# Attention layers of a one-core kernel: the second half of the key projection moves from PSUM bank 7 to bank 4

## The chip, the cores and the metric

The kernel runs on one core of a Trainium2 chip. The metric is the device time of one execution in microseconds (us). TensorE (PE in the profile; its weight loads are PEld) does the matrix products and writes PSUM; VectorE (DVE), ScalarE (ACT) and GpSimd (POOL) do the rest; SyncE (SP) issues the transfers. PSUM is used here as eight banks of 128 x 512 float32, written `PS[:, bank, :]`.

## The reference

The input x is 64 sequences of 64 tokens of 256 channels. Four residual layers follow one another: two of attention with style modulation, then two state-space layers. The change touches the attention layers only:

```
x  = x * s1;  x = (x - mean(x)) * rsqrt(var(x) + 1e-5)
q, k, v = x @ q_weight.T * q_dc, x @ k_weight.T * k_dc, x @ v_weight.T * v_dc * s2
attn = softmax(q @ k.T * 16 ** -0.5)        # 16 heads of 16, 64 x 64 per sequence
x  = x + (attn @ v) @ w_weight.T * w_dc + v_flat @ u_weight.T * u_dc
```

## The kernel before, in words

Channels lie on the partitions, in two halves of 128 (`HC` = 2, index m or c). Tokens are worked in groups of 8 sequences, 512 tokens (one PSUM bank wide). There are 8 groups and two attention layers, so `body` runs 16 times; call the turns 0 to 15. Turns 1 to 4 are a loop on the chip that is entered twice with two bodies each time round, and so are 9 to 12; the others are written out. The two state-space layers come after turn 15 and are not touched.

Each engine has a written-out order, and semaphores hold the engines together. One turn of `body` on TensorE does, for group `it`: the outward projection of the group before; the turned values; the scores of the second half; then eight times "turn" (transpose a block of probabilities into PSUM, bank 4 for even k and bank 7 for odd k, `turn_bank`, line 253) and "weigh" (probabilities by values, bank 5). ScalarE copies each turned block to SBUF (`turned`, line 649). In the middle of these eight, TensorE prepares other groups:

- `mean_spread(it + 2, 7)` spreads the token means of group it + 2 into bank 7; VectorE subtracts them (`centred`, line 1347, tile xm). xm is complete when that bank has been read.
- the key projection of group it + 1 (`project(one, 1, m, ...)`, line 881): first half to bank 6, second half to bank 7. Since bank 7 holds the means until `centred` is through, the second half waits for xm.
- ScalarE reads each half twice, once for each parity of the heads (`keys`, line 637, tile kz), after it has done the exponent of the second half (line 653) and the squares of group it + 2 (line 625).
- the query projection of group it + 1: its halves go to banks 6 and 7 again, so each waits until `keys` has read that half's bank.
- `square_sums(it + 2, 6)`, the skip projection (line 881 on vsc, banks 2 and 3), `rstd_spread(it + 2, 7)`, `turn(it, 4)` and so on.

A float32 projection of one half is two matmul calls and shows as four matmul records in the trace ("x4"); both halves together are "x8". Turn 14 prepares no group it + 2 (there is no group 16), so there the second half of the keys has no xm to wait for. Turn 15 makes no projections of keys.

The last step of a turn is `project(one, 2, 1, ...)`, the second half of the values; ScalarE copies it, takes the exponent of the next group's first scores, and VectorE sums, scales and adds the residual of the group before (lines 1377 to 1410).

Of the kernel before, what the change touches and what calls it, by code (L numbers as in the profile page):

```python
# [14 lines left out]
HC, DC = H // P, DI // P  # L15
# [27 lines left out]
def cond_resid_kernel(nc, xT, condT, attw, win, wconv, chan, wxp, wdt, dtv, wout, dskip,  # L43
                      ident_d, spread_d, fold_d, masks_d, rowmask_d, ones_x, out):
    f32, bf16 = mybir.dt.float32, mybir.dt.bfloat16
    ALU, ACT, AX = mybir.AluOpType, mybir.ActivationFunctionType, mybir.AxisListType
# [15 lines left out]
    with es:  # L62
# [5 lines left out]
        def sb(name, shape, dt=f32, where=None):  # L68
            return (where or es).enter_context(nc.sbuf_tensor(name, shape, dt))

        PS = es.enter_context(nc.psum_tensor("PS", [P, 8, 512], f32))
# [13 lines left out]
        par = [masks[:, 0:1], masks[:, 1:2]]  # L85
# [23 lines left out]
        kz = sb("kz", [P, HC, 2, TOK], where=att)  # L109
# [141 lines left out]
        fin = sem("final")  # L251

        turn_bank = (4, 7) * 4
        AT = LAYERS * G
        USED, READY, KEPT, W0 = 16, 20, 2, 32
        Y_STORES = PASSES * (CHUNKS // 2) * 16
# [230 lines left out]
        def _(pl):  # L487
# [14 lines left out]
            def body(it, g, after):  # L502
                for r in range(2):
                    pl.wait_ge(rcp_r, it * 2 + r + 1)
                    pl.tensor_tensor(late_half(ex, r), late_half(ex, r), rs[:, r, :].rearrange("p (j e) -> p j e", j=4)[:, :, 4:8]  # L505
                                     .unsqueeze(3).broadcast_to([P, 4, 4, S]), ALU.mult).then_inc(pn_r, 1)
                pl.wait_ge(t2_r, it * 2 + 2)
                pl.tensor_tensor(t3[:, :, :], X[:, ds(g, 1), :, :].rearrange("p a c t -> p (a c) t"), t2[:, :, :],
                                 ALU.add).then_inc(t3_r, 1)
                if after:  # L510
                    skip_values(it + 1, *after)

            skip_values(0, 0, 0)
            for l in range(LAYERS):
# [4 lines left out]
                for g in range(5, G):  # L519
                    n = l * G + g + 1  # L520
                    body(l * G + g, g, (n // G, n % G) if n < AT else None)

# [74 lines left out]
        def _(act):  # L597
# [35 lines left out]
            def keys(n):  # L633
                for c in range(HC):
                    act.wait_ge(k_mm, n * 2 + c + 1)
                    for e in range(2):
                        act.activation(kz[:, c, e, :], PS[:, 6 + c, :], ACT.Copy, scale=par[e]).then_inc(k_r, 1)

            def values(n, c):
                act.wait_ge(v_mm, n * 2 + c + 1)  # L640
# [22 lines left out]
            def body(it, one, two):  # L663
                exponent(it, 0)
                for b2 in range(4):
                    by_parity(it, b2)
                turned(it, 0)
                turned(it, 1)
                if two:
                    mean(it + 2, 6)  # L670
                turned(it, 2)
                turned(it, 3)
                exponent(it, 1)
                if two:
                    squares(it + 2)
                if one:
                    keys(it + 1)
                if two:
                    deviation(it + 2, 6)
                turned(it, 4)  # L680
                if one:
                    values(it + 1, 0)
                for k in range(5, 8):
                    turned(it, k)
                if one:
                    values(it + 1, 1)
# [15 lines left out]
            for l in range(LAYERS):  # L702
# [6 lines left out]
                for g in range(5, G):  # L709
                    it = l * G + g  # L710
                    body(it, it + 1 < AT, it + 2 < AT)

# [165 lines left out]
        def _(pe):  # L878
            def project(l, w, m, rhs, bank, done):
                for c in range(HC):  # L880
                    mm = pe.matmul(PS[:, bank, :], Wl[l][:, w, c, m * P:(m + 1) * P], rhs[:, c, :],  # L881
                                   start=(c == 0), stop=(c == HC - 1))
                mm.then_inc(done, 1)
# [33 lines left out]
            def square_sums(n, bank):  # L917
                pe.wait_ge(sq_r, n + 1)
                sums(sq, bank, var_r)
# [25 lines left out]
            def turn(it, k):  # L945
                for j in range(4):
                    mm = pe.transpose(PS[:, turn_bank[k], j * P:(j + 1) * P],  # L947
                                      ex[:, k // 4, j, (k % 4) * P:(k % 4 + 1) * P], ident[:, :])
                mm.then_inc(pt_mm, 1)
# [13 lines left out]
            def outward_att(it, l):  # L963
                pe.wait_ge(av_r, it * 2 + 2)
                for m in range(HC):
                    project(l, 3, m, av, turn_bank[m], w_mm)

            def body(it, l, par_n, before, one, two):
                x1 = xn[:, 1 - par_n, :, :]
                if before is not None:  # L970
                    outward_att(it - 1, before)
                pe.wait_ge(v_r, it * 2 + 2)
                turn_values(it, 0)
                turn_values(it, 1)
                if before is None:
                    dcoef(1, range(2), 4, 7)
                pe.wait_ge(sub_r, it * 2 + 1)
                scores(it, 1)
                for b2 in (2, 3):
                    pe.wait_ge(vbd_r, it * 8 + 2 * b2 - 2)  # L980
                    turn_values(it, b2)
                if before is None:
                    dcoef(1, range(2, 5), 4, 7)
                    pe.wait_ge(dco_e, LAYERS * 2)
                else:
                    pe.wait_ge(t1_r, it * 2 - 1)
                pe.wait_ge(pe_r, it * 2 + 1)
                turn(it, 0)
                if before is not None:
                    pe.wait_ge(t1_r, it * 2)  # L990
                turn(it, 1)
                pe.wait_ge(vbd_r, it * 8 + 8)
                if two:
                    mean_sums(it + 2, 6)
                weigh(it, 0)
                pe.wait_ge(pn_r, it * 2 + 1)
                turn(it, 2)
                weigh(it, 1)
                turn(it, 3)
                weigh(it, 2)  # L1000
                weigh(it, 3)
                if two:
                    mean_spread(it + 2, 7)
                if one is not None:
                    pe.wait_ge(xn_r, it + 2)
                    project(one, 1, 0, x1, 6, k_mm)
                    if two:
                        pe.wait_ge(xm_r, it + 3)
                    project(one, 1, 1, x1, 7, k_mm)
                    for m in range(HC):  # L1010
                        pe.wait_ge(k_r, it * 4 + 2 * m + 6)
                        project(one, 0, m, x1, 6 + m, q_mm)
                if two:
                    pe.wait_ge(q_r, it * 2 + 3)
                    square_sums(it + 2, 6)
                pe.wait_ge(sub_r, it * 2 + 2)
                pe.wait_ge(vs_r, it + 1)
                for m in range(HC):
                    project(l, 4, m, vsc, 2 + m, u_mm)
                if one is not None:  # L1020
                    pe.wait_ge(q_r, it * 2 + 4)
                if two:
                    rstd_spread(it + 2, 7)
                pe.wait_ge(pe_r, it * 2 + 2)
                turn(it, 4)
                if one is not None:
                    project(one, 2, 0, x1, 6, v_mm)
                if two:
                    pe.wait_ge(xn_r, it + 3)
                turn(it, 5)  # L1030
                if one is not None:
                    pe.wait_ge(t2_r, it * 2 + 2)
                    scores(it + 1, 0)
                pe.wait_ge(av_r, it * 2 + 1)
                weigh(it, 4)
                pe.wait_ge(pn_r, it * 2 + 2)
                turn(it, 6)
                weigh(it, 5)
                turn(it, 7)
                weigh(it, 6)  # L1040
                weigh(it, 7)
                if one is not None:
                    pe.wait_ge(v_r, it * 2 + 3)
                    project(one, 2, 1, x1, 6, v_mm)
# [13 lines left out]
            pe.wait_ge(xn_r, 1)  # L1058
            x0 = xn[:, 0, :, :]
            for m in range(HC):  # L1060
                project(0, 1, m, x0, 6 + m, k_mm)
            square_sums(1, 0)
            for m in range(HC):
                pe.wait_ge(k_r, 2 * m + 2)
                project(0, 0, m, x0, 6 + m, q_mm)
            rstd_spread(1, 1)
            pe.wait_ge(q_r, 2)
# [6 lines left out]
            for l in range(LAYERS):  # L1074
# [4 lines left out]
                for g in range(5, G):  # L1079
                    it = l * G + g  # L1080
                    body(it, l, it % 2, l, (it + 1) // G if it + 1 < AT else None, it + 2 < AT)
            outward_att(AT - 1, LAYERS - 1)

# [232 lines left out]
        def _(v):  # L1316
# [164 lines left out]
            for l in range(LAYERS):  # L1481
# [7 lines left out]
                for g in range(5, G):  # L1489
                    it = l * G + g  # L1490
                    body(it, l, g, it % 2, (l, g - 1), ((it + 1) // G, (it + 1) % G) if it + 1 < AT else None,
                         (it + 2) % G if it + 2 < AT else None)
            for c in range(HC):
# [293 lines left out]
```

## Time and profile before

| what | value |
|---|---|
| median of 3 runs | 2034.54 us (2029.61 to 2037.28) |
| profiled execution | 2042.08 us |
| its span, first to last instruction | 2040.3 us |
| mean granted TensorE clock | 0.961 of full |
| PE busy | 1783.1 us, 87% of the span |
| DVE busy | 1706.3 us, 84% |
| ACT busy | 1327.3 us, 65% |
| POOL busy | 658.3 us, 32% |

Attention takes about the first 620 us of the span, the state-space layers the rest. A row of the timeline gives the start and the duration in us, the engine, the line and operation, out<-in, the number of instructions merged, and in brackets the idle time of that engine before it with what ended it. A row of a table by stretch ends with the granted TensorE clock as a share of full speed (1.00 is 2.4 GHz, 0.50 is 1.2 GHz), the DMA share and GB/s.

### The profile page before, as it was taken

How to read it: one execution, taken by the hardware profiler on the slowest of the kernel's cores; microseconds unless marked ns; L12 is line 12 of the kernel's file. 1: busy time of each engine (PE TensorE's matmuls, PEld its weight loads, DVE VectorE, ACT ScalarE, POOL GpSimd, SP SyncE). 2: the span in 40 equal slices, each digit the busy share in tenths (PEclk: the TensorE clock that was granted, in tenths of full speed). 3: DMA queues.
4: the chain of work that ended last, by engine and by line, in shares of the span. 5: the costliest groups of instructions: out<-in, count | busy, mean ns of one | idle time of the engine just before them, and what ended most of it. 6: DMA issues, size and time to landing. Idle time of an engine off the chain costs nothing.

```text
span 2040.3 us, 46458 instructions
## 1 busy us (share of the span) xinstructions
PE 1783.1 (87%) x15152; PEld 853.0 (42%) x15152; DVE 1706.3 (84%) x2508; ACT 1327.3 (65%) x2180; POOL 658.3 (32%) x592
## 2 busy tenths in 40 slices
PE   7899898998988787788998997987787889899978
PEld 5555455555544545442222223444454322222234
DVE  4778878787776898989999996668888899999965
ACT  4545445454443778698998992048776899899910
POOL 0233223332222011434765660001014356656500
PEclk9999999999998898979999999999998899999999
DMA  3000000000000333354554746712333545546477
GB/s 145 2 2 0 1 2 28 2 1 0 1 2 32 121 110 138 109 180 135 175 160 123 248 145 212 219 50 104 129 129 118 173 138 173 159 155 225 145 220 270
DMA packets 127179, 228.29 MB, mean 112 GB/s; under 512 B 36084, under 2 KB 61812, under 8 KB 118004
## 3 DMA queue, kind: packets, MB, share of 16 engines
q1 hardware_dynamic: 127064, 226.80, 34.1%
q8 instruction: 66, 1.08, 0.2%
q14 instruction: 49, 0.40, 0.1%
HBM read 143.40 MB, written 83.36 MB: 111 GB/s over the span
## 4 chain that ended last, share of the span: by engine, by line
PE 57%; DVE 18%; ACT 11%; issue 7%; DMA 4%; SPq 2%; DVEq 0%; ACTq 0%; POOL 0%; POOLq 0%
PE PS L1237 12%; PE PS L1254 12%; PE PS L1095 9%; PE PS L881 8%; DMA yt<-y_d 3%; DVE q L1669 3%; ACT ex L653 3%; DVE ex L1371 3%; PE PS L1257 3%; PE PS L1304 2%; PE PS L1148 2%; PE PS L947 2%; DVE sm L1377 2%; DVE mx L1367 2%; DVE z L1557 2%
## 5 line engine op out<-in xcount | busy, mean ns | idle before, releaser
L866 ACT ACTIVATE R<-q,Ast 128x512 f32<-128x512 f32 x1024 | 637.7, 709 | 42.3 <-DVE q L1669 29.6
L1669 DVE SCALAR_TENSOR_TENSOR q<-R,PS 128x512 f32<-128x512 f32 x1008 | 612.0, 705 | 20.4 <-PE PS L1237 10.1
L548 POOL TENSOR_TENSOR Uw<-Ub,rowmask 96x512 bf16<-96x512 bf16 x256 | 338.9, 1357 | 193.9 <-PE PS L1237 181.3
L1237 PE MATMUL PS<-xq,Uw 97*128 97x512 bf16 x1024 | 323.7, 394 | 53.4 <-DVE q L1669 39.3
L1254 PE MATMUL PS<-q,Wy 128*32 128x512 f32 x2016 | 284.7, 618 | 0.8 <-DVE q L1669 0.7
L539 POOL TENSOR_TENSOR xlo<-xr,xmi 128x512 bf16<-128x512 f32 x64 | 72.3, 1161 | 529.3 <-ACT xmi L791 529.3
L1237 PEld LDWEIGHTS PS<-xq,Uw 97*128 97x128 bf16 x1024 | 85.7, 97 | 366.6 <-DVE q L1669 321.2
L1095 PE MATMUL PS<-X,Win 128*128 (+1 forms) x512 | 232.0, 603 | 4.3 <-DVEq L1501 2.9
L881 PE MATMUL PS<-xn,Wl 128*128 128x512 f32 x384 | 185.4, 614 | 25.8 <-DVE xm L1347 19.0
L505 POOL TENSOR_TENSOR ex<-ex,rs 128x1024 f32<-128x1024 f32 x32 | 94.1, 2941 | 206.1 <-DVE rs L1380 206.1
L649 ACT ACTIVATE pT<-PS 128x512 f32<-128x512 f32 x128 | 75.3, 596 | 119.1 <-PE PS L947 118.9
L1095 PEld LDWEIGHTS PS<-X,Win 128*128 128x128 f32 x512 | 95.3, 193 | 112.2 <-issue 109.4
L1528 DVE SCALAR_TENSOR_TENSOR acc<-xp,Wc,acc 128x512 f32<-128x512 f32 x192 | 137.5, 780 | 2.0
L1304 PE MATMUL PS<-yg,Wo 128*128 128x512 f32 x256 | 114.4, 602 | 0.0
L881 PEld LDWEIGHTS PS<-xn,Wl 128*128 128x128 f32 x384 | 68.0, 193 | 107.8 <-issue 53.3
L1257 PE MATMUL PS<-xq,By 96*32 96x512 bf16 x1024 | 112.0, 387 | 0.0
L1367 DVE TENSOR_REDUCE mx<-PS 128x32 f32<-128x2048 f32 x32 | 73.1, 2285 | 43.2 <-PE PS L931 43.2
L1148 PE MATMUL PS<-ident,z 128*128 128x128 f32 x256 | 53.8, 377 | 53.2 <-DVE sg L1541 53.2
L762 ACT ACTIVATE z<-z,Ch 128x512 f32<-128x512 f32 x64 | 43.0, 720 | 87.7 <-DVE z L1557 87.7
L653 ACT ACTIVATE ex<-ex 128x2048 f32<-128x2048 f32 x32 | 61.1, 1909 | 51.9 <-DVE ex L1371 50.9
L498 POOL TENSOR_TENSOR vsc<-vTd,vs_t 128x1024 f32<-128x1024 f32 x16 | 41.1, 2569 | 157.6 <-ACT vTd L641 157.6
L947 PE MATMUL PS<-ident,ex 128*128 128x128 f32 x512 | 80.6, 284 | 10.8 <-DVE ex L1383 9.9
(151 smaller groups left out, 2744.5 us busy)
## 6 DMA issues: line engine op xcount, KB each, us to landing
xq<-xpart_d SPq DMA_DIRECT2D x384, 192.0 KB
sg_d<-sg SPq DMA_DIRECT2D x16, 1024.0 KB, 4.2
xn_d<-z SPq DMA_DIRECT2D x16, 1024.0 KB, 4.0
y_d<-ys SPq DMA_DIRECT2D x64, 256.0 KB, 3.9
xnp<-xn_d SPq DMA_DIRECT2D x16, 1024.0 KB, 6.6
sgp<-sg_d SPq DMA_DIRECT2D x16, 1024.0 KB, 9.1
yt<-y_d SPq DMA_DIRECT2D x32, 512.0 KB, 10.0
xpart_d<-xh SPq DMA_DIRECT2D x16, 512.0 KB, 2.9
```

Of the source, the lines that this page charges most:

```text
L548: pl.tensor_tensor(Uw[0:XROWS, h, w, :, :, :], Ub[0:XROWS, w, 0:N, ds(s0, CH)].rearrange("p n t -> p t n").unsqueeze(2).broadcast_to([XROW ...
L653: act.activation(ex[:, r, :, :], ex[:, r, :, :], ACT.Exp).then_inc(exp_r, 1)
L866: act.activation(R[:, w, :], q[:, t % 2, w, :], ACT.Relu, scale=Ast[:, h, w, t:t + 1], bias=CLIP).then_inc(ac_r, 1)
L881: mm = pe.matmul(PS[:, bank, :], Wl[l][:, w, c, m * P:(m + 1) * P], rhs[:, c, :], start=(c == 0), stop=(c == HC - 1))
L947: mm = pe.transpose(PS[:, turn_bank[k], j * P:(j + 1) * P], ex[:, k // 4, j, (k % 4) * P:(k % 4 + 1) * P], ident[:, :])
L1095: mm = pe.matmul(PS[:, m % DC, :], Win[:, c, m * P:(m + 1) * P], X[:, ds(g, 1), c, :].rearrange("p a t -> p (a t)"), start=(c == 0), stop= ...
L1237: pe.matmul(PS[:, w, :], Uw[0:KROWS, h, w, t, :, :].rearrange("p b n -> p (b n)"), xq[0:KROWS, hb, w, s8 % XT, :], start=True, stop=True). ...
L1254: pe.matmul(PS[32 * w:32 * w + 32, 4 + h, :], Wy[:, h, w, t * 32:(t + 1) * 32], R[:, w, :] if last else q[:, s8 % 2, w, :], start=(t == 0) ...
L1257: mm = pe.matmul(PS[32 * w:32 * w + 32, 4 + h, :], By[0:XROWS, h, t, w, MID - t * GB:MID + (CH - t) * GB], xq[0:XROWS, hb, w, xt, :], star ...
L1304: mm = pe.matmul(PS[:, 4 + 2 * u + m, :], Wo[:, c, m * P:(m + 1) * P], yg[:, u, c, :], start=(c == 0), stop=(c == DC - 1))
L1528: v.scalar_tensor_tensor(out=tiled(acc[:, m, :]), in0=xp[:, m, :, j:j + S], scalar=Wc[:, m, j:j + 1], in1=tiled(acc[:, m, :]), op0=ALU.mul ...
L1669: v.scalar_tensor_tensor(out=q[:, s8 % 2, w, :], in0=R[:, w, :], scalar=2 * CLIP, in1=PS[:, w, :], op0=ALU.min, op1=ALU.subtract).then_inc ...
```

## The change

The second half of the key projection goes to bank 4, where the turned probabilities of k = 2 stood, which ScalarE has copied out by then. The wait for xm no longer stands ahead of it; it stands ahead of the second half of the queries, which still goes to bank 7. The first half of the queries waits, as before, until both reads of the keys' first half are done. The second half of the queries waits for no read of keys any more; instead `turn(it, 4)`, the next writer of bank 4, waits for all four. The same is done ahead of the loop for group 0.

```
+        key_bank = (6, 4)
@@ keys, ScalarE
-   act.activation(kz[:, c, e, :], PS[:, 6 + c, :], ACT.Copy, scale=par[e]).then_inc(k_r, 1)
+   act.activation(kz[:, c, e, :], PS[:, key_bank[c], :], ACT.Copy, scale=par[e]).then_inc(k_r, 1)
@@ body, TensorE
                     pe.wait_ge(xn_r, it + 2)
-                    project(one, 1, 0, x1, 6, k_mm)
+                    for m in range(HC):
+                        project(one, 1, m, x1, key_bank[m], k_mm)
+                    pe.wait_ge(k_r, it * 4 + 6)
+                    project(one, 0, 0, x1, 6, q_mm)
                     if two:
                         pe.wait_ge(xm_r, it + 3)
-                    project(one, 1, 1, x1, 7, k_mm)
-                    for m in range(HC):
-                        pe.wait_ge(k_r, it * 4 + 2 * m + 6)
-                        project(one, 0, m, x1, 6 + m, q_mm)
+                    project(one, 0, 1, x1, 7, q_mm)
...
                 pe.wait_ge(pe_r, it * 2 + 2)
+                if one is not None:
+                    pe.wait_ge(k_r, it * 4 + 8)
                 turn(it, 4)
@@ ahead of the loop, TensorE
-                project(0, 1, m, x0, 6 + m, k_mm)
+                project(0, 1, m, x0, key_bank[m], k_mm)
             square_sums(1, 0)
+            pe.wait_ge(k_r, 2)
             for m in range(HC):
-                pe.wait_ge(k_r, 2 * m + 2)
                 project(0, 0, m, x0, 6 + m, q_mm)
```

On TensorE, in the loop's body, the stretch of keys and queries stood in this order before. PS is PSUM, xn the normalized group, Wl the weights of the layer; k_ready counts ScalarE's reads of keys, xm_ready VectorE's `centred`.

```order
L881 MATMUL PS<-xn,Wl 128x512 [waits xn_ready]
L881 MATMUL PS<-xn,Wl 128x512
L881 MATMUL PS<-xn,Wl 128x512 [waits xm_ready]
L881 MATMUL PS<-xn,Wl 128x512
L1011 ISA
L881 MATMUL PS<-xn,Wl 128x512 [waits k_ready]
L881 MATMUL PS<-xn,Wl 128x512
L1011 REGISTER_ALU
L881 MATMUL PS<-xn,Wl 128x512 [waits k_ready]
L881 MATMUL PS<-xn,Wl 128x512
```

And it stands so now (lines are one higher):

```order
L882 MATMUL PS<-xn,Wl 128x512 [waits xn_ready]
L882 MATMUL PS<-xn,Wl 128x512 x3
L1009 ISA
L882 MATMUL PS<-xn,Wl 128x512 [waits k_ready]
L882 MATMUL PS<-xn,Wl 128x512
L882 MATMUL PS<-xn,Wl 128x512 [waits xm_ready]
L882 MATMUL PS<-xn,Wl 128x512
```

The four matmuls of the keys follow one another without a wait; the wait for xm has moved behind the first half of the queries, and the second wait for k_ready is gone from here.

Further on in the same body on TensorE, from the spread of the inverse deviations to the fifth turn, it read before:

```order
L906 MATMUL PS<-rstd,spread 128x128 [waits rstd_ready]
L906 MATMUL PS<-rstd,spread 128x128 x3
L947 MATMUL PS<-ident,ex 128x128 [waits probs_early]
L947 MATMUL PS<-ident,ex 128x128 x3
L881 MATMUL PS<-xn,Wl 128x512 x2
```

and now:

```order
L907 MATMUL PS<-rstd,spread 128x128 [waits rstd_ready]
L907 MATMUL PS<-rstd,spread 128x128 x3
L1027 REGISTER_ALU [waits probs_early]
L948 MATMUL PS<-ident,ex 128x128 [waits k_ready]
L948 MATMUL PS<-ident,ex 128x128 x3
L882 MATMUL PS<-xn,Wl 128x512 x2
```

One register instruction has come in ahead of the fifth turn, with the wait for the keys' reads behind it; one went from the stretch above.

## Rows read from the trace of the kernel before

**Rows 1.** Page, part 1: busy time of each engine.
```profile
PE 1783.1 (87%) x15152; PEld 853.0 (42%) x15152; DVE 1706.3 (84%) x2508; ACT 1327.3 (65%) x2180; POOL 658.3 (32%) x592
```

**Rows 2.** Chain of waits, 278 to 318 us: start, us, what.
```profile
282.70 1.91 ACT ex L653
284.61 0.95 ACT sq L625
285.56 1.17 ACT kz L637 x2
286.72 0.04 issue
286.77 3.70 PE PS L881 x8
...
304.47 1.02 ACT vTd L641
305.51 1.92 ACT ex L653
```

**Rows 3.** Timeline of PE in turn 6, 280 to 296 us.
```profile
280.99 1.88 PE L881 MATMUL PS<-xn,Wl 128*128 128x512 f32 x4
284.45 1.98 PE L881 MATMUL PS<-xn,Wl 128*128 128x512 f32 x4 [1.58 <-DVE xm L1347]
286.77 3.70 PE L881 MATMUL PS<-xn,Wl 128*128 128x512 f32 x8 [0.33 <-ACT kz L637]
...
295.40 0.60 PE L947 MATMUL PS<-ident,ex 128*128 128x128 f32 x4
```

**Rows 4.** Timeline of DVE and ACT in the same stretch.
```profile
282.70 1.91 ACT L653 ACTIVATE ex<-ex 128x2048 f32<-128x2048 f32 x1 [3.13 <-DVE ex L1371]
283.19 1.21 DVE L1347 TENSOR_TENSOR xm<-xs,PS 128x1024 f32<-128x1024 f32 x1
284.52 1.04 ACT L625 ACTIVATE sq<-xm 128x1024 f32<-128x1024 f32 x1
285.47 2.40 ACT L637 ACTIVATE kz<-PS,masks 128x512 f32<-128x512 f32 x4
```

**Rows 5.** Source line 1347: who waited for it (us, times).
```profile
  PE PS L881: 19.0, 12
```

**Rows 6.** Timeline of PE in turn 14, 568 to 582 us.
```profile
569.01 3.70 PE L881 MATMUL PS<-xn,Wl 128*128 128x512 f32 x8
574.97 5.40 PE L881 MATMUL PS<-xn,Wl 128*128 128x512 f32 x8 [2.25 <-ACT kz L637]
580.20 3.60 PE L881 MATMUL PS<-vsc,Wl 128*128 128x512 f32 x8
```

**Rows 7.** Table by stretch; the granted clock is third from the end.
```profile
90.00:126.00 36.00, 33.01 (x392) 19.42 (x392) 28.23 (x26) 17.09 (x27) 10.84 (x5) 1.00 0.01 1
280.00:287.00 7.00, 5.08 (x22) 2.47 (x18) 6.68 (x6) 4.30 (x5) 0.00 (x0) 1.00 0.00 0
287.00:294.00 7.00, 7.00 (x31) 3.02 (x31) 4.49 (x8) 1.55 (x4) 2.94 (x1) 1.00 0.00 0
571.00:575.30 4.30, 2.05 (x5) 0.70 (x5) 2.92 (x3) 3.45 (x4) 0.00 (x0) 1.00 0.01 2
575.40:578.70 3.30, 3.30 (x5) 1.35 (x4) 2.52 (x4) 0.67 (x2) 2.15 (x1) 0.50 0.00 0
578.90:582.00 3.10, 3.10 (x9) 1.41 (x8) 0.92 (x2) 0.00 (x0) 0.58 (x1) 1.00 0.00 0
240.90:244.20 3.30, 3.30 (x48) 2.35 (x40) 3.30 (x2) 1.14 (x3) 0.08 (x1) 0.50 0.00 0
```

**Rows 8.** Timeline of PE: other long idle gaps in attention.
```profile
89.90 1.17 PE L947 MATMUL PS<-ident,ex 128*128 128x128 f32 x8 [1.78 <-DVE ex L1383]
239.36 1.17 PE L947 MATMUL PS<-ident,ex 128*128 128x128 f32 x8 [1.95 <-DVE ex L1383]
607.05 6.59 PE L881 MATMUL PS<-vsc,Wl 128*128 128x512 f32 x8 [2.79 <-DVE ex L1371]
```

**Rows 9.** Timeline of PE ahead of the turns, and in turn 0.
```profile
31.87 3.70 PE L881 MATMUL PS<-xn,Wl 128*128 128x512 f32 x8
60.05 7.42 PE L881 MATMUL PS<-xn,Wl 128*128 128x512 f32 x16
```

## The prediction

> **What bounds the kernel now.** I read the page's busy times first: TensorE is busiest with 87% of the span [rows 1], but that mean covers four layers, and the change is in the first 620 us. So I read the chain of waits inside one attention turn, then the timeline of the engines that meet in it.
>
> Turn 6 stands for its kind. The chain [rows 2] runs over ScalarE's exponent of the second scores at 282.70, the squares, two of the four reads of the keys, and then over TensorE from 286.77, where the queries start, until ScalarE's copy of the values at 304.47 and the next exponent at 305.51. So what sets the start of the queries is ScalarE, and from there on TensorE's own work is the path.
>
> TensorE's timeline [rows 3] shows the place of the change: first half of the keys at 280.99, an idle gap of 1.58 us that ends with VectorE's xm, second half at 284.45, a gap of 0.33 us that ends with ScalarE's kz, queries at 286.77. It happens in 12 of the 16 turns: line 1347 is what TensorE waited for 12 times, 19.0 us in all [rows 5], and 12 x 1.58 = 19.0. These are turns 1 to 4 and 6 to 13. In turn 0 keys and queries run as one piece of sixteen without a gap [rows 9].
>
> **The change part by part.**
>
> *The wait for xm ahead of the keys' second half goes.* The second half follows the first at once. Turn 14, where no xm is awaited, shows both halves back to back: 3.70 us [rows 6]. In turn 6 they would end at 280.99 + 3.70 = 284.69 instead of 286.43 (284.45 + 1.98, rows 3), 1.74 us earlier. What is late next? ScalarE reads the first half from 285.47, right behind the squares, and the second from the middle of its 2.40 us, about 286.67 [rows 4]. Both halves are ready for it before and after. Its reads are held by its own order, exponent 282.70, squares 284.52, keys 285.47, with nothing idle between. So the reads move by nothing.
>
> *The first half of the queries* still needs bank 6, which these reads free. It starts at 286.77, as now. The gain from the first edit up to here is 0 us, not 19.0; all that happened is that TensorE's idle time has become one piece, 284.69 to 286.77 = 2.08 us, where it was 1.58 and 0.33 with 1.98 us of matmuls between them. That piece is where I look for the cost, below.
>
> *The second half of the queries* waits for xm instead of for kz. xm is done at 283.19 + 1.21 = 284.40, its turn comes about 1.85 us after 286.77, at 288.6; the reads of keys that it awaited before ended at 285.47 + 2.40 = 287.87. Neither is late: 0 us. Ahead of the turns, in row 31.87, the queries run in one piece of 3.70 us with the old wait in it [rows 9], so that edit too is worth 0 us.
>
> *The new wait ahead of the fifth turn.* It is satisfied at 287.87 and stands ahead of an instruction at 295.40 [rows 3, 4], 7.5 us of slack; behind it are queued the first half of the values and the next scores. One register instruction is added there, one taken out between the two halves of the queries. Both spots show no idle time now. The nearest price is the 0.04 us of "issue" in the chain [rows 2]: bounds +0.04 x 12 = 0.5 us and minus the same. I take 0.
>
> *The clock in the longer gap.* The trace grants TensorE 1.00 through turn 6, in the gaps as in the queries behind them, and through turn 1 [rows 7]. In turn 14 it does not. There the same eight matmuls of keys stand without a hole, then an idle gap of 2.25 us, then the same eight of queries: full clock up to 575.30, 0.50 from 575.40 to 578.70, full again from 578.90 [rows 7]. The queries took 5.40 us where turn 6 shows 3.70 [rows 3, 6]: 1.70 us for one fall. This is exactly the order the change makes in twelve more turns, with a gap of 2.08 us in place of 2.25.
>
> Is 2.08 us enough? The clock fell behind a gap of 1.95 us at 239.36 (0.50 from 240.90, rows 7), and behind 2.79 us at 607.05, where eight matmuls took 6.59 us, 2.89 more than 3.70 [rows 8]. It did not fall behind 1.78 us at 89.90, whose stretch shows 1.00, nor in the twelve gaps of 1.58. So of the gaps of 1.95 us and longer that these rows show all three were followed by half clock, and of those of 1.78 and shorter none; 2.08 is on the falling side. The work around the 1.95 us gap was short transposes, though, not these long matmuls, so I don't count on every turn. I take ten falls of twelve, my choice between the bounds of 0 and 12. From 286.77 to 304.47 TensorE is the path and no other engine's slack absorbs a slower query [rows 2], so each fall counts in full.
>
> The Trainium skill, "TensorE: Matmul & The Clock Gate", section "A second HAM failure mode: psum-queue depth-cycling", says that idling between groups of matmuls while cycling through PSUM banks can make the clock swing between its two levels; by that the cost above is to be expected, and turn 14 agrees (0.50 behind the 2.25 us gap). The same page's "HAM oscillation — how this bites in real kernels" gives as its abstract rule a warning only against idle gaps longer than any of these; by it nothing falls and the time stays where it is. Here the trace disagrees, since the clock fell behind 2.25 us.
>
> **The sum.** 10 x 1.70 = +17.0 us, everything else 0. On the profiled execution's own time, 2042.08 (span 2040.3 and 1.8 around it), that is 2059.1. This execution lies 7.5 us above the median of the three timed runs, 2034.54, and above the highest, 2037.28, so I put the sum on the median: 2051.5 us. The forecast's own range: eight falls (+13.6) to twelve (+20.4), with the 3 to 5 us that the timed runs spread around their median: 2045 to 2058.
>
> **The rivals.**
>
> - *Nothing falls; no change.* All edits are worth 0 as worked out, and the clock holds through a 2.08 us gap as it did through 1.78. For it: dense matmuls on both sides, twelve shorter gaps without a fall. Against it: turn 14, the same sequence, fell. Time 2034.5. The page's abstract rule comes to the same.
> - *Fewer falls.* Some four of twelve: +6.8, 2041.3. For it: only one fall of exactly this shape is on record. It decides whether the result can be told from no change.
> - *The gain the wait seems to promise; faster.* If the 1.58 us that TensorE waits for xm were on the path, 12 x 1.58 = 19.0 us would go: 2015.5. Its place is the start of the queries, and it decides only if kz ended earlier than now, that is if ScalarE's reads were held by the keys' second half. Against it: kz stands without idle time behind the squares [rows 4], and the chain doesn't pass through xm into TensorE [rows 2].
> - *Longer falls.* If the clock stayed low as long as behind 607.05 (2.89 us lost), 12 x 2.89 = 34.7: 2069. Against it: behind 575.40, with these very matmuls, it was back within 3.5 us.
>
> **How the numbers follow.** Forecast (eight to twelve falls) 0.76; no fall 0.12; fewer falls 0.07; longer falls 0.02; faster 0.03. A measurement of this kernel tells about 0.5% from no change, 10.2 us, which is six falls. Of the forecast 0.74 is beyond it, and the longer falls: slower 0.76. No fall, fewer falls and the rest: same 0.21. Faster 0.03. The range goes from 2036, inside the cases of few falls, to 2058, which leaves out about 0.17: most of the case without a fall and the two outer rivals.
>
> **What would show it.** In the profile after, in turn 6: the keys as one x8 of 3.70 us, behind it an idle gap of about 2.1 us ended by kz, no wait for xm on TensorE; ScalarE's kz still 0.95 us behind the start of the squares. The queries at 5.3 to 5.4 us instead of 3.70 in about ten of the twelve turns, with the clock at 0.50 there, and a turn of 37.8 us in place of 36.1. The mean granted clock of such a turn's stretch at about 0.95 in place of 1.00 (half clock from 575.40 to 578.70 is 3.3 us of 36, rows 7); idle time elsewhere as now. If the queries stay at 3.70 us at full clock, the price of the gap is wrong; if kz starts earlier than 0.95 us behind the squares' start, or the queries start earlier than kz's second read, the zero of the gain is wrong; if idle time appears ahead of the fifth turn, the zero of the new wait is.

## The result: 1% slower, and the profile after

The changed kernel took 2055.24 us (median of 4 runs, 2050.78 to 2058.24), the kernel before 2035.91 (4 runs). The ratio is 1.0098 with a 95% interval of 1.0068 to 1.0128, that is +14 to +26 us. A second, longer comparison (below) gave 1.0073, 1.0058 to 1.0088. The forecast was 2051.5 us, between 2036 and 2058. Three executions are left out of all ratios below as far slower than the rest: one of experiment 3 (5737 us, unexplained) and two of the kernel before beside experiments 5 and 8 (2118.92 and 2178.28 us, at a mean granted clock of 0.83 and 0.79).

The profiled execution took 2050.78 us. It happened to be the fastest of the four, while that of before was above all three timed runs of its page; so the two spans lie only 8.6 us apart (2048.9 against 2040.3), and I compare stretches of them, not the spans. The first matmul of the state-space layers starts at 625.32 us before and at 637.66 after: +12.3 us within attention. The layers behind it, which the change does not touch, happened to take 3.7 us less than in the profile of before.

In what follows, a fall is a stretch in which the granted clock of TensorE goes from 1.00 to 0.50 and back, and a gap is time in which TensorE idles.

The page's first part of the changed kernel, to be held against [rows 1]. Its columns are the same.

```profile
PE 1790.8 (87%) x15152; PEld 856.8 (42%) x15152; DVE 1706.9 (83%) x2508; ACT 1327.7 (65%) x2180; POOL 658.5 (32%) x592
```

The instructions are as many as before, TensorE's matmuls are 7.7 us longer busy and its weight loads 3.8 us; no other engine is longer busy by more than 0.6. Nothing was added; the same instructions of TensorE got slower.

The chain of waits of turn 6 in the changed kernel (start, us, what), the piece that answers to [rows 2]:

```profile
286.62 1.91 ACT ex L654
288.53 0.95 ACT sq L626
289.48 1.16 ACT kz L638 x2
290.64 0.04 issue
290.69 5.40 PE PS L882 x8
296.08 0.57 PE PS L901 x16
296.66 3.63 PE PS L882 x8
```

Each link that [rows 2] has too lasts as long as there, to 0.01 us, but for the queries: 5.40 us in place of 3.70.

The timeline of TensorE in that turn, which answers to [rows 3], and ScalarE's and VectorE's beside it, which answer to [rows 4]:

```profile
284.90 3.60 PE L882 MATMUL PS<-xn,Wl 128*128 128x512 f32 x8
290.69 5.40 PE L882 MATMUL PS<-xn,Wl 128*128 128x512 f32 x8 [2.18 <-ACT kz L638]
...
287.10 1.21 DVE L1350 TENSOR_TENSOR xm<-xs,PS 128x1024 f32<-128x1024 f32 x1
288.44 1.04 ACT L626 ACTIVATE sq<-xm 128x1024 f32<-128x1024 f32 x1
289.39 2.40 ACT L638 ACTIVATE kz<-PS,masks 128x512 f32<-128x512 f32 x4
```

The keys now run as one piece. From their start to that of the queries it is 5.79 us (284.90 to 290.69), before it was 5.78 (280.99 to 286.77): not a hundredth gained. kz starts 0.95 us behind the squares, as before. And the wait for xm is gone for TensorE: line 1350 has only this left under "who waited for it", where [rows 5] had TensorE 12 times.

```profile
  ACT sq L626: 3.1, 2
```

The clock of that turn, table by stretch (clock third from the end), for [rows 7]:

```profile
284.00:290.00 6.00, 4.50 (x16) 2.24 (x16) 5.71 (x5) 3.38 (x4) 0.00 (x0) 1.00 0.00 0
290.20:293.50 3.30, 2.81 (x4) 1.27 (x5) 2.23 (x3) 1.59 (x3) 2.18 (x1) 0.59 0.00 0
360.00:372.00 12.00, 9.82 (x41) 4.40 (x41) 9.72 (x11) 5.84 (x8) 2.94 (x1) 1.00 0.00 0
```

The third row is turn 8, where the clock did not fall. TensorE's timeline, the queries of four turns:

```profile
136.24 5.40 PE L882 MATMUL PS<-xn,Wl 128*128 128x512 f32 x8 [2.18 <-ACT kz L638]
174.12 5.40 PE L882 MATMUL PS<-xn,Wl 128*128 128x512 f32 x8 [2.18 <-ACT kz L638]
...
366.17 3.70 PE L882 MATMUL PS<-xn,Wl 128*128 128x512 f32 x8 [2.18 <-ACT kz L638]
402.25 5.40 PE L882 MATMUL PS<-xn,Wl 128*128 128x512 f32 x8 [2.18 <-ACT kz L638]
```

Twelve turns have the gap of 2.18 us. In nine the queries are slow (turns 2 to 4, 6, 7, 9 to 12), in three they are not (1, 8, 13). From one turn's queries to the next, turn 6 with its fall takes 37.78 us (290.69 to 328.47) and turn 8 without one 36.08 (366.17 to 402.25): 1.70 apart. Nine falls of 1.70 are 15.3 us. The queries of turn 1 start 1.2 us earlier than before, for what lies ahead of them, and those of turn 14 start 14.0 later: 15.2 between. Turn 14 itself, whose clock fell before [rows 6], shows this time:

```profile
588.97 3.70 PE L882 MATMUL PS<-xn,Wl 128*128 128x512 f32 x8 [2.26 <-ACT kz L638]
```

1.7 us back: 14.0 less 1.7 is the 12.3 us measured at the end of attention.

One more fall stands in this part of the profile, early in turn 5, and not behind one long gap. It comes between short matmuls, behind gaps of 1.58 and 1.25 us:

```profile
237.27 1.42 PE L932 MATMUL PS<-kz,qs 32*64 32x128 f32 x64 [1.58 <-DVE ex L1374]
239.94 1.97 PE L942 MATMUL PS<-ident,vTd 128*128 128x128 f32 x8 [1.25 <-ACT vbd L660]
```
```profile
239.60:242.90 3.30, 1.97 (x8) 1.56 (x8) 3.23 (x3) 2.70 (x7) 0.95 (x1) 0.50 0.00 0
```

The first two rows are TensorE's timeline, the third the table by stretch. In the profile of before the eight transposes of line 942 (941 there) take 1.38 us, behind the same two gaps, and the clock falls only at 240.9, behind the next gap of 1.95. The fall in the changed kernel, though it came earlier, lengthened nothing more: from the queries of turn 4 to those of turn 5 it is 42.58 us (212.01 to 254.59) against 40.88 before (209.80 to 250.68), and the 1.70 between them are the slow queries of turn 4 themselves.

### The profile page after: what moved, and what is told of

Its sections match the earlier page's. It is cut to its first block, busy times and chain, and to the rows that moved or that the text cites. A ratio compares the mean times of both kernels' runs of the same rounds, so it can differ in the third digit from the quotient of the medians.

```text
span 2048.9 us, 46464 instructions
## 1 busy us (share of the span) xinstructions
PE 1790.8 (87%) x15152; PEld 856.8 (42%) x15152; DVE 1706.9 (83%) x2508; ACT 1327.7 (65%) x2180; POOL 658.5 (32%) x592
## 4 chain that ended last, share of the span: by engine, by line
PE 51%; DVE 20%; ACT 14%; issue 9%; DMA 4%; SPq 1%; DVEq 1%; POOL 0%; ACTq 0%; POOLq 0%
PE PS L1257 9%; PE PS L882 9%; PE PS L1098 9%; PE PS L1240 8%; ACT R L867 4%; DVE q L1672 4%; DMA yt<-y_d 3%; ACT ex L654 3%; DVE ex L1374 3%; PE PS L1307 2%; PE PS L1260 2%; PE PS L1151 2%; PE PS L948 2%; DVE sm L1380 2%; DVE mx L1370 2%
## 5 line engine op out<-in xcount | busy, mean ns | idle before, releaser
L1672 DVE SCALAR_TENSOR_TENSOR q<-R,PS 128x512 f32<-128x512 f32 x1008 | 610.0, 676 | 19.9 <-ACT R L867 7.9
L882 PE MATMUL PS<-xn,Wl 128*128 128x512 f32 x384 | 193.9, 645 | 30.4 <-ACT kz L638 30.3
L882 PEld LDWEIGHTS PS<-xn,Wl 128*128 128x128 f32 x384 | 73.1, 204 | 115.7 <-issue 71.0
```

Source lines behind the costliest of these rows:

```text
L1672: v.scalar_tensor_tensor(out=q[:, s8 % 2, w, :], in0=R[:, w, :], scalar=2 * CLIP, in1=PS[:, w, :], op0=ALU.min, op1=ALU.subtract).then_inc ...
```

## The experiments

All were timed beside the kernel before; ratios are to it, with a 95% interval.

**1. The changed kernel once more.** No edit.

> The changed kernel once more, for its time on this chip and a second profile. Theory (the clock falls behind the longer idle gap ahead of the queries): again slower, by 8 to 12 falls of 1.70 us, +14 to +20 us over the kernel before; in its profile the turns whose queries take about 5.4 us are those with half clock, and they need not be the same turns as in the first profile. Rival (the new bank itself costs, by reads of bank 4 beside writes of bank 6): the queries are slower in all twelve turns alike, at full clock.

Ratio 1.0073 (1.0058 to 1.0088), median 2053.42 against 2038.81: +14.9 us. In its profile the queries are slow in turns 2, 3, 6 to 11 and 13, fast in 4, 12 and 14. So the places of the falls change from one execution to the next, with the same gap, as the clock theory allows and a cost of the bank does not. Turn 1 is a case by itself, in TensorE's timeline:

```profile
90.49 1.76 PE L948 MATMUL PS<-ident,ex 128*128 128x128 f32 x8 [1.78 <-DVE ex L1386]
...
101.81 3.70 PE L882 MATMUL PS<-xn,Wl 128*128 128x512 f32 x8 [0.72 <-ACT kz L638]
```

and its table by stretch:

```profile
90.30:93.60 3.30, 3.11 (x40) 2.60 (x40) 3.16 (x4) 1.46 (x3) 1.81 (x1) 0.56 0.00 0
```

The clock fell here behind the gap of 1.78 us that stands in the kernel before too [rows 8] and that had passed at full clock there. I had taken that row for a gap that is safe; it is not. This fall cost nothing: from line 948 to the queries it is 11.32 us here (90.49 to 101.81) as in the first profile (88.72 to 100.04), where the clock held. TensorE was slower, but the queries waited for kz in both.

**2. The wait for xm put back, new banks kept.**

```
-                    for m in range(HC):
-                        project(one, 1, m, x1, key_bank[m], k_mm)
+                    project(one, 1, 0, x1, key_bank[0], k_mm)
+                    if two:
+                        pe.wait_ge(xm_r, it + 3)
+                    project(one, 1, 1, x1, key_bank[1], k_mm)
```

> The changed kernel with the wait for xm put back ahead of the keys' second half; banks 6 and 4 and the new wait ahead of the fifth turn stay. Clock theory: the gap is 1.58 and 0.33 us again with the matmuls between, no fall in the twelve turns, 0 us (within 3) against the kernel before. Rival (the bank or the new wait costs): it stays slower by 14 to 20 us.

Ratio 1.0001 (0.9989 to 1.0013). Bank 4, and the wait and register instruction ahead of the fifth turn, cost nothing that shows, within 2.7 us. The whole loss hangs on when the second half of the keys runs. The kernel waits more and is 15 us faster.

**3. Needless work in the gap.**

```
                     for m in range(HC):
                         project(one, 1, m, x1, key_bank[m], k_mm)
+                    if two:
+                        pe.wait_ge(xm_r, it + 3)
+                        for c in range(HC):
+                            pe.matmul(PS[:, 7, :], Wl[one][:, 1, c, 0:P], x1[:, c, :],
+                                      start=(c == 0), stop=(c == HC - 1))
```

> The changed kernel with needless work in the gap: behind the keys and the wait for xm, one more projection of 1.7 us into bank 7, which nobody reads and which the queries' second half overwrites. No output changes. Clock theory: 2.2 us of idle time become about 0.4, no fall, the queries at 3.70 us from the same place behind kz; 0 us (within 3) against the kernel before, so 14 to 20 us faster than the changed kernel although it does 13 projections more. Rival (bank or wait costs): slower than before by 14 to 20 us, plus whatever the added work costs.

Ratio 1.0001 (0.9989 to 1.0013). TensorE's timeline in turn 6, the added work at line 1012:

```profile
283.16 3.60 PE L882 MATMUL PS<-xn,Wl 128*128 128x512 f32 x8
286.62 1.98 PE L1012 MATMUL PS<-xn,Wl 128*128 128x512 f32 x4
288.93 3.70 PE L882 MATMUL PS<-xn,Wl 128*128 128x512 f32 x8 [0.33 <-ACT kz L638]
```

and over turns 6 to 13, a table by stretch: first this kernel, then the changed one.

```profile
280.00:560.00 280.00, 268.80 (x3040) 156.49 (x3039) 219.05 (x194) 135.21 (x212) 82.55 (x30) 1.00 0.02 6
```
```profile
280.00:560.00 280.00, 254.35 (x2881) 148.81 (x2882) 213.70 (x188) 133.04 (x210) 81.10 (x30) 0.96 0.02 6
```

The queries start 5.77 us behind the keys' start, as before, and take 3.70 us. This is the sharpest of the tests. The keys still run as one piece, and the wait for xm that comes with the added work holds up nothing that the timeline shows (xm is complete at 286.56, the added work starts at 286.62). Work is only added, and the loss is gone, with the clock at 1.00 over the eight turns in place of 0.96.

**4. Half of that work** (one matmul of 512 columns instead of two; `range(1)` in the lines above).

> The changed kernel with half the needless work of the run before in the gap: one matmul of 512 columns, about 0.86 us, behind the keys, so that some 1.3 us stay idle ahead of the queries. Clock theory: an idle stretch no longer than those of before (1.58 us) brings no fall: 0 us (within 3) against the kernel before. Rival (any undivided hole of this kind brings some falls, in proportion to its length): 1.3 of 2.2 us, +8 to +10 us.

Ratio 0.9998 (0.9985 to 1.0011); the gap is 1.19 us in each of the twelve turns and none fell.

**5. A sliver of it** (that one matmul cut to 128 columns).

> The changed kernel with a sliver of needless work in the gap: one matmul of 128 columns behind the keys, about 0.1 to 0.2 us, so that some 2.0 us stay idle. Theory (what decides is how long the engine idles ahead of the queries): nearly as bad as the changed kernel, +10 to +20 us. Rival (it is the missing interruption of the gap that counts, any work behind the keys cures it): 0 us.

Ratio 1.0046 (1.0029 to 1.0063): +9.4 us, between the two. The theory's lower end was +10, the rival's 0 is excluded. The gap is 1.83 us and not 2.0, since even the sliver holds the engine about 0.35. TensorE's timeline in turns 7 and 8:

```profile
326.36 3.70 PE L882 MATMUL PS<-xn,Wl 128*128 128x512 f32 x8 [1.83 <-ACT kz L638]
...
362.44 5.40 PE L882 MATMUL PS<-xn,Wl 128*128 128x512 f32 x8 [1.83 <-ACT kz L638]
```

Five of eleven such gaps fell (turn 1 had again fallen earlier); 5 x 1.70 = 8.5 us. Together, falls ahead of the queries of turns 1 to 4 and 6 to 13:

| idle ahead of the queries | falls |
|---|---|
| 0.33 us (before, experiments 2 and 3) | 0 of 36 |
| 1.19 to 1.24 us (experiments 4 and 7) | 0 of 24 |
| 1.83 us (experiment 5) | 5 of 11 |
| 2.18 us (changed kernel, two profiles) | 18 of 23 |

The first line had a gap of 1.58 us a little earlier in the kernel before and in experiment 2, between the long matmuls of the keys, which brought no fall in 24 turns either. The counts hold for this place only: turn 14 is not among them (its gap of 2.25 to 2.26 us was followed by a fall in 2 of the 9 profiles that have it), nor is the start of turn 5, where the clock fell behind gaps of 1.58 and 1.25 us in the changed kernel. And neighbouring turns are not independent draws, since the falls come in rows (turns 6 to 11 in experiment 1).

**6. Useful work in the gap.** The first half of the skip projection, from behind the sums of squares.

```
                         project(one, 1, m, x1, key_bank[m], k_mm)
+                    pe.wait_ge(sub_r, it * 2 + 2)
+                    pe.wait_ge(vs_r, it + 1)
+                    project(l, 4, 0, vsc, 2, u_mm)
                     pe.wait_ge(k_r, it * 4 + 6)
...
-                pe.wait_ge(sub_r, it * 2 + 2)
-                pe.wait_ge(vs_r, it + 1)
-                for m in range(HC):
-                    project(l, 4, m, vsc, 2 + m, u_mm)
+                if one is None:
...
+                    project(l, 4, 0, vsc, 2, u_mm)
+                project(l, 4, 1, vsc, 3, u_mm)
```

> The changed kernel with useful work in the gap: the first half of the skip projection (1.72 us), which stands behind the sums of squares, goes between the keys and the queries' wait for kz. Theory: no fall, and TensorE's path behind the queries is shorter by 1.72 us in each of the turns 0 to 14 where the gap takes it, 12 to 13 of them: -20 us against the kernel before (2014 to 2018). In turns 0 and 5 there is little or no gap, so nothing is gained there. Rival (behind the queries something else is on the path, such as the inverse deviations that VectorE makes for the spread): between -5 and 0 us.

Ratio 0.9892 (0.9874 to 0.9909), 2016.98 us: -22.0. And the same in the kernel before, between the two halves of the keys:

> The kernel before, banks and waits as they were, with the first half of the skip projection moved between the two halves of the keys, into the 1.58 us gap that waits for xm. Theory (the idle time ahead of the queries can be used with either bank; only its filling counts): 1.72 us less behind the queries in twelve turns, the keys' second half later by some 0.1 us only: -20 us, the same as with the new bank within 3 us. Rival (the new bank is what makes the gap usable): -10 us or less.

Ratio 0.9893 (0.9876 to 0.9910): -21.8, no different. The 1.58 us were usable all along, and the bank change is not needed for it. The turn is 34.60 us long in both (for instance 341.02 to 375.62, and 338.99 to 373.59, from one spread of the means to the next) against 36.10 before (352.16 to 388.26). That is 1.50 us, not the 1.72 moved. The rest seems to have gone into a new wait. The timeline of turn 6, with the new bank (VectorE and TensorE):

```profile
284.33 0.29 DVE L1341 SCALAR_TENSOR_TENSOR rstd<-vare,rstd 128x128 f32<-128x128 f32 x1
284.77 1.13 PE L907 MATMUL PS<-rstd,spread 128*128 128x128 f32 x8
```

TensorE's skip half, 282.80 and four records of 0.43, is through at about 284.5; the spread starts at 284.77, behind VectorE's end at 284.62. The timeline names no releaser for it, so this wait is my reading. 12 x 1.50 = 18.0; turn 14 gets the 1.72 too, and where its clock used to fall, its gap, now 0.54 us, no longer brings that (1.70). That is 19.7 to 21.4 of the 22.

**7. ScalarE's reads of keys ahead of the squares**, in the changed kernel and in the one before.

```
-                if two:
-                    squares(it + 2)
                 if one:
                     keys(it + 1)
+                if two:
+                    squares(it + 2)
```

> The changed kernel with ScalarE's order turned round: the four reads of keys go ahead of the squares of group it + 2. The keys of both halves are in PSUM by then, so kz starts 0.95 us earlier and so do the queries, and the idle gap is 2.2 - 0.95 = 1.2 us. Theory: no fall, and 12 x 0.95 = 11 us less: -11 us against the kernel before (-8 to -13). It would be slower than that if the squares, now behind the reads, come late for the sums of squares (they need to be done 3.6 us behind the queries' start and are done about 2.2 behind it). Rival (the path isn't ScalarE's order but something behind the queries): 0 us.

> The kernel before with the same turn of ScalarE's order. There the keys' second half still ends about 1.7 us later than with the new bank (286.4 in turn 6), but the queries' first half waits for the reads of the first half only, which could end at 285.85. TensorE is in the second half of the keys until then. Theory: queries start at about 286.2 in place of 286.77, 0.5 us less in twelve turns, -6 us (-3 to -9), about half of what the same edit brings with the new bank. Rival (the bank makes no difference to this edit): the same -11 us as with the new bank, or 0 in both.

With the new bank 0.9931 (0.9915 to 0.9948), -14 us; with the old 0.9947 (0.9931 to 0.9963), -11. The turn lengths fit better than the totals: 35.14 and 35.49 us against 36.10, so 0.96 and 0.61 us a turn where 0.95 and 0.5 were expected; both totals lie 3 to 5 us beyond what was expected. The turn lengths explain up to 1 of it. Turn 14 gives 1.7 more against the profile of before: its queries take 3.70 us in both profiles here and took 5.40 there. The rest is within the intervals' 3 us or so on each side. Here the bank is worth something: VectorE's xm holds the keys' second half in the old kernel, and the queries queue behind it. The difference of 0.35 us a turn is 4 us, and the intervals overlap.

**8. Both edits together**, with the new bank and the old.

> The changed kernel with both useful edits: the first half of the skip projection in the gap, and ScalarE's reads of keys ahead of the squares. Keys and skip half need 5.3 us on TensorE without a hole, so the queries can start at about 0.5 us earlier than with the skip half alone, not 0.95. Theory: the gains are bounded by TensorE from here on: -20 us of the skip half and 12 x 0.4 = -5 more, -25 us against the kernel before (2012 to 2016). Rival (they add in full): -22 - 14 = -36 us.

> The kernel before (keys' second half in bank 7, behind xm) with the same two edits. Here the keys' second half can't start before xm, so TensorE's work ahead of the queries ends at the same place as with the new bank, 5.3 us of work from the same start with 0.0 to 0.1 us idle. ScalarE's reads of the second half come later, but the queries' first half does not wait for them. Theory: the bank is worth nothing here either, -25 us, equal to the run above within 3 us. Rival (the keys' second half, 1.7 us later, delays the squares behind ScalarE's reads and with them the sums): 3 to 8 us slower than the run above.

0.9845 (0.9824 to 0.9867), 2006.37 us against 2040.39, with the new bank; 0.9859 (0.9838 to 0.9881), 2009.74 us, with the old. The first is the best version found, 1.5% faster than the kernel before and 2.3 to 2.5% faster than the changed one. TensorE's timeline of it in turn 6 shows why there is nothing left to fill at this place:

```profile
272.53 3.60 PE L882 MATMUL PS<-xn,Wl 128*128 128x512 f32 x8
275.97 1.88 PE L882 MATMUL PS<-vsc,Wl 128*128 128x512 f32 x4
277.69 3.60 PE L882 MATMUL PS<-xn,Wl 128*128 128x512 f32 x8
281.21 0.64 PE L901 MATMUL PS<-sq,ones_h 128*32 128x128 f32 x16
```

Keys, skip half and queries without idle time. -31.6 us is more than the -25 expected and less than the rival's -36: the turn is 33.87 us (339.27 to 373.14), 12 x 2.23 = 26.8 less, where I had counted on 25, and turn 14's 1.7 to 3.4 us, which I had left out in these expectations, make up most of the rest. With the old bank it is 34.00 us a turn, -28.8 us in all; the two differ by 3 us, inside their intervals.

## Why the prediction was right

*The start of the queries doesn't move: right, to 0.01 us.* 5.79 us behind the keys' start against 5.78; TensorE no longer waits for xm; kz at the same distance. The gain of 19.0 us which the wait for xm promised was 0.

*The new wait, the register instruction and the bank cost 0: right.* Experiment 2 measured them together at 0 within 2.7 us.

*The idle time in one piece costs clock: right, and shown.* The queries take 5.3 to 5.4 us in the turns where they are slow, and the clock falls there. Filling the gap with work cures it (experiments 3 and 4), and so does cutting it up as before (experiment 2). The gap was 2.18 us where the sum had 2.08: the x8 of turn 14 shows as 3.70 and that of the keys here as 3.60.

*1.70 us for one fall: right* (5.40 less 3.70). *Ten falls of twelve: nearly.* Nine in the first profile; in the second nine of the eleven where the clock still stood at full, with one earlier fall in turn 1. 18 of 23 is 78%, so 9.4 of twelve, +16 us. The two measurements are +19.9 and +14.9 on the ratio; neither interval excludes the forecast's +17.0.

*The evidence for it was weaker than it looked.* I read the rows as if a length divided the gaps into those that bring a fall and those that don't: 1.95 and more yes, 1.78 and less no. The runs don't bear that out. The clock fell behind a gap of 1.78 us in experiment 1, behind gaps of 1.83 five times of eleven, and at the start of turn 5 of the changed kernel behind 1.58 and 1.25, while my row of 1.95 us stands right behind two such gaps, which I did not show. The gap of 2.25 us in turn 14, which was my pattern and gave the price, was followed by a fall in the profile of before and in that of experiment 2, and in none of the seven others that have it. At the place of the change falls are more frequent behind the longer gap (5 of 11 at 1.83 us, 18 of 23 at 2.18), but the length of a single gap does not decide. The price of 1.70 us was read off correctly; that the page of before showed a fall behind turn 14's gap at all was luck, and ten of twelve was a choice without a count behind it that came out near.

*The rivals.* No fall at all and a gain are excluded by both measurements. The longer falls (2.89 us) did not occur at this place: every slow row there shows 5.3 to 5.4 us. The Trainium skill's rule for PSUM-queue cycling ("TensorE: Matmul & The Clock Gate", "A second HAM failure mode: psum-queue depth-cycling") puts the swings of the clock down to idling between groups of matmuls, and the runs agree with that part: the clock swung here behind such idle time. The runs give the bank no part in it: experiment 2 keeps the new bank and shows no loss.

What stays open: why a given turn falls and its neighbour, with the same gap to 0.01 us, does not. The runs show that it differs between executions, and no experiment here controls it.

## What to carry to other kernels

Before removing a wait, ask whether it is the last one ahead of the next work on the path; here the wait behind it, for kz, ended as late as before, and the engine only finished early and then idled in one long piece instead of two short ones. On TensorE that is not neutral: here an undivided gap of about 2 us ahead of long matmuls cost 1.7 us each time that the clock fell behind it, which was three times of four. Look first for useful work that fits in such a gap; moving half a projection there was worth 22 us, with either bank. And don't take one profile for the habit of the clock: a gap that passes at full clock in one execution can bring a fall in the next.

## What the runs showed of the hardware

- Adding fourteen projections of 1.7 us (turns 0 to 13; 24 us of TensorE's time, the expectation had counted thirteen) made the changed kernel 15 us faster.
- A fall behind the gap ahead of the queries cost 1.6 to 1.7 us, whatever the gap: 5.3 to 5.4 us in place of 3.70 behind 1.83, 2.18 and 2.25 us. Elsewhere it cost another sum. Behind the 2.79 us gap of turn 15, eight matmuls of the same size took 5.24 us in experiment 3 and 6.63 in the changed kernel; and falls where the queries waited for ScalarE anyway (turn 5 of the changed kernel, turn 1 of experiment 1) cost nothing.
- The clock also fell behind short gaps with short matmuls between them: 1.58 and 1.25 us, at 239.6 us in the changed kernel.
- The bank of the keys' second half made no difference: 0 within 2.7 us for bank 4 against 7 (experiment 2).
